# Loading the input batch by batch and re-planning the opening of a four-block transformer kernel on one core

## The chip, the cores and the metric

The kernel runs on one NeuronCore of a Trainium2 chip. TensorE (PE) multiplies matrices into PSUM; VectorE (DVE), ScalarE (ACT) and GpSimd (POOL) do the elementwise work; SyncE (SP) only issues DMA transfers. Each engine works off its own list of instructions in a fixed order and waits at semaphores. The metric is the device time of one execution in microseconds (us), lower is better.

## The reference, cut to what matters

The input `x` is (8, 256, 288): 8 batches of 256 tokens. Three transformer blocks follow each other, each with a condition vector `c` that gives six rows per batch (shift, scale and gate, twice), and a rotation closes:

```python
mod = silu(c) @ w_adaln + b_adaln                     # 6 rows of 288 per batch
sh_msa, sc_msa, g_msa, sh_mlp, sc_mlp, g_mlp = split(mod, 6)
h = ln(x) * (1 + sc_msa) + sh_msa
qkv = h @ w_qkv + b_qkv                               # 16 heads of 18
x = x + g_msa * (softmax(q k / sqrt(18)) v @ w_proj + b_proj)
h = ln(x) * (1 + sc_mlp) + sh_mlp
x = x + g_mlp * mlp(h)        # block 0: 4 experts, top 2; blocks 1 and 2: one MLP
...
U, _ = qr(P)                  # P is (288, 64)
R = expm(A(silu(c) @ W.T + b))# A skew-symmetric, 64x64, one per batch
out = x + ((x U) R - x U) U^T
```

Nothing before the second layer norm mixes batches, so batch 0 can go through its first attention while the input of batch 7 is still in HBM.

## The kernel before, in words

Activations stay in SBUF for the whole run: `X` holds the 16 tiles of 128 tokens (two tiles are one batch), `XT` the transposed and modulated copy as an f16 high part and an f16 low part. Weights are loaded as f32 into one of seven staging buffers (`STG`; four of them lie in the memory of `H`, so the trace calls them `H` early in the program), and ACT (`w_hi`, L2037 and L2042) and DVE (`w_lo`, L1679 and L1686) split them into high and low parts (`WQ`, `WP`, `WG`, `W`).

The program is written by a planner that runs when the kernel is built. Generators for the parts of the work (`prep`: layer norm, modulation, QKV; `maxima_rows`: row maxima of the scores, by DVE; `attend`; `settle` and `finish`; the MLP stream; `householder`: 64 reflections for the QR, one after another; `ada` and `vrows`: the rows from the condition vector) call `do(lane, kind, cost, ...)`, which appends a step to an engine's list. `deal` picks which generator goes on. Then `by_readiness` re-orders the steps of each engine: a model clock per engine, an assumed cost per step, and a tail after a step's end at which its result is there. For DMA steps this tail came from a table of constants, `LANDS` (6.0 us for a reload of saved weights, 7.5 us for `x_in`, 5.0 us for a weight block, 2.2 us for anything else), whatever else was in flight. On the chip only the resulting order counts.

The opening, with the lines of the trace: ACT's queue issues `x` in four transfers of two batches each (L2028). SP issues the condition vector (`c_in`, L2284), the first pair of 288-column groups of `w_adaln` (`cond_in`, L2292, bias L2295), `w_qkv` (`w_in`, L2306 to L2311), `P` transposed (`p_in`, L2287, tile `AT`), and the second pair of groups. PE's first instruction is the transposition of row 0 of the Householder reflections (L1566, reads `AT`), then the products of the condition rows (L1406), whose sums DVE adds (`cond_add`, L1673), PE transposes (L1399) and ACT copies to `SC` (L2062). POOL writes the identity and masks (`consts`), DVE writes constants in two steps: `xt_ones` (L1661 to L1667, which ACT's first activation waits for) and `dconsts` (L1638 to L1658: identity in f16, zeroed `QB`, `KB`, `WP1`, `V32`, columns of ones). The layer norm of a batch is BN_STATS (L1734) and BN_AGGR (L1739) on DVE, power on POOL, scaling on ACT (L2086, L2087), six transpositions on PE (L1416, L1417), modulation (`full`, L1715 on DVE) and split into `XT` (L1721 to L1730). The QKV products are L1389, seven f16 products per tile and third.

## Time and profile before

| | before |
|---|---|
| median of 3 runs | 1450.6 us (1448.38 to 1451.12) |
| the profiled execution's own time | 1447.77 us |
| its span in the trace | 1446.0 us |
| PE busy | 1337.2 us (92%) |
| DVE busy | 902.2 us (62%) |
| ACT busy | 788.8 us (55%) |
| POOL busy | 419.1 us (29%) |
| mean granted TensorE clock | 0.967 |

The span runs from the first to the last recorded instruction; the execution's own time has 1.8 us more around it. A busy PE counts a matmul at whichever clock was granted, so busy time is not work at full speed.

### The profile page before, as it was taken

The page shows a single profiled execution, that of the slowest core. Times are in us where ns is not written, and L with a number is a line of the kernel's source. Part 1 is how long each engine was busy: PE and PEld are TensorE (multiplying, and loading weights), DVE is VectorE, ACT ScalarE, POOL GpSimd, SP SyncE. Part 2 cuts the span into 40 slices and gives each one's busy share as a digit, 9 for nine tenths or more (in the row PEclk, how much of TensorE's full clock was granted, in tenths as well). Part 3 has the DMA queues.
Part 4 walks back from the last instruction along what each step waited for, and adds up shares of the span by engine and source line. Part 5 has one row for each costly group of instructions (what it writes and reads, how often), then busy time and mean ns, then how long its engine had stood idle before and what let it go on. Part 6 is the DMA issues. An engine that isn't in the chain of part 4 may idle for free.

```text
span 1446.0 us, 30299 instructions
## 1 busy us (share of the span) xinstructions
PE 1337.2 (92%) x11841; PEld 813.3 (56%) x11841; DVE 902.2 (62%) x1985; ACT 788.8 (55%) x1563; POOL 419.1 (29%) x805
## 2 busy tenths in 40 slices
PE   2777999899999999999999999989999999999978
PEld 1444555556567565665655665546656565555545
DVE  4678776776855655575447564584858755766442
ACT  2466677566754534454435343465655775755622
POOL 1213243242431334323343233221313323231110
PEclk8787999999999999999999999999999999999989
DMA  5114224534212312132212213141000130000000
GB/s 156 46 37 143 75 76 157 153 122 141 80 31 73 73 51 81 25 64 85 81 40 55 77 42 122 58 92 51 1 13 6 30 88 5 22 10 22 14 25 17
DMA packets 76738, 91.80 MB, mean 63 GB/s; under 512 B 38989, under 2 KB 69814, under 8 KB 73270
## 3 DMA queue, kind: packets, MB, share of 16 engines
q1 hardware_dynamic: 74486, 87.52, 20.8%
q10 hardware_dynamic: 2112, 2.36, 0.6%
q8 instruction: 94, 1.54, 0.4%
q14 instruction: 46, 0.38, 0.1%
HBM read 73.22 MB, written 16.38 MB: 62 GB/s over the span
## 4 chain that ended last, share of the span: by engine, by line
PE 79%; DVE 6%; issue 5%; ACT 4%; DMA 3%; SPq 2%; POOL 1%; POOLq 0%; DVEq 0%; ACTq 0%
PE P L1389 33%; PE P L1549 7%; PE P L1550 7%; PE P L1551 7%; PE P L1518 4%; DVE NM L1819 3%; PE P L1509 2%; PE P L1566 2%; PE P L1416 2%; PE P L1485 2%; PE P L1406 2%; PE P L1494 1%; PE P L1546 1%; PE P L1472 1%; PE P L1560 1%
## 5 line engine op out<-in xcount | busy, mean ns | idle before, releaser
L1389 PE MATMUL P<-XT,W 128*128 128x512 f16 x1512 | 350.7, 383 | 7.6 <-DVE XT L1730 4.8
L2246 POOL TENSOR_TENSOR X<-X,TM 128x288 f32<-128x288 f32 x144 | 123.6, 860 | 532.6 <-DVE TM L1894 340.8
L1549 PE MATMUL P<-W,H 128*128 128x288 f16 x864 | 248.3, 287 | 0.4 <-issue 0.3
L1550 PE MATMUL P<-W,H 128*128 128x288 f16 x864 | 248.0, 287 | 0.0
L1551 PE MATMUL P<-W,H 128*128 128x288 f16 x864 | 248.0, 287 | 0.0
L1389 PEld LDWEIGHTS P<-XT,W 128*128 128x128 f16 x1512 | 141.3, 98 | 179.7 <-issue 22.8
L2165 ACT ACTIVATE G<-P 128x512 f32<-128x512 f32 x216 | 128.9, 597 | 140.5 <-PE P L1389 131.0
L2155 ACT ACTIVATE ARENA<-P 128x512 f32<-128x512 f32 x256 | 136.0, 599 | 102.8 <-PE P L1509 102.1
L1819 DVE TENSOR_REDUCE NM<-P 128x2 f16<-128x512 f32 x256 | 159.9, 687 | 11.1 <-PE P L1494 10.5
L1389 PE MATMUL P<-WQ,XT 128*128 128x288 f16 x1008 | 143.9, 295 | 10.2 <-issue 5.3
L1888 DVE TENSOR_TENSOR H<-G,H 128x512 f16<-128x512 f32 x139 | 97.9, 708 | 85.3 <-ACT H L2166 85.2
L2251 POOL TENSOR_TENSOR H<-G,H 128x512 f16<-128x512 f32 x77 | 93.2, 1214 | 184.1 <-ACT H L2166 183.7
L2166 ACT ACTIVATE H<-P 128x512 f16<-128x512 f32 x216 | 128.5, 595 | 0.0
L1389 PEld LDWEIGHTS P<-WQ,XT 128*128 128x128 f16 x1008 | 96.6, 100 | 49.2 <-issue 21.3
L1549 PEld LDWEIGHTS P<-W,H 128*128 128x128 f16 x864 | 84.7, 98 | 27.7 <-issue 7.6
L1551 PEld LDWEIGHTS P<-W,H 128*128 128x128 f16 x864 | 84.7, 98 | 21.5
L1550 PEld LDWEIGHTS P<-W,H 128*128 128x128 f16 x864 | 84.7, 98 | 20.9
L2171 ACT ACTIVATE HQS<-P 64x288 f32<-64x288 f32 (+31 forms) x64 | 23.9, 374 | 119.8 <-PE P L1566 119.8
L1894 DVE SCALAR_TENSOR_TENSOR TM<-P,CW,G 128x288 f32<-128x288 f32 x64 | 32.9, 514 | 65.1 <-PE P L1551 64.7
L1518 PE MATMUL P<-ARENA,V 128*32 128x256 f32 x1024 | 71.3, 388 | 0.4 <-ACT ARENA L2155 0.3
L2080 ACT ACTIVATE FULL<-P,SC 128x256 f32<-128x256 f32 (+1 forms) x90 | 43.5, 557 | 41.2 <-PE P L1417 41.2
L1566 PE MATMUL P<-AT,IDF 64*64 64x288 f32 (+42 forms) x128 | 44.0, 426 | 23.7 <-DMA AT<-in_PT 16.9
(306 smaller groups left out, 2170.2 us busy)
## 6 DMA issues: line engine op xcount, KB each, us to landing
W<-scr_w SPq DMA_DIRECT2D x9, 1440.0 KB, 6.1
W<-scr_w SPq DMA_DIRECT2D x9, 1368.0 KB, 5.8
scr_w<-W SPq DMA_DIRECT2D x4, 1440.0 KB, 5.7
scr_w<-W SPq DMA_DIRECT2D x4, 1368.0 KB, 5.7
STG<-in_L_w SPq DMA_DIRECT2D x8, 576.0 KB, 5.1
STG<-in_L_w SPq DMA_DIRECT2D x9, 432.0 KB, 4.5
STG<-in_L_WT SPq DMA_DIRECT2D x11, 324.0 KB, 4.3
G<-scr_ada SPq DMA_DIRECT2D x24, 144.0 KB, 3.6
```

What stands on the lines that cost most here:

```text
L1389: ins = e.matmul(o, l, r, start=k == 0, stop=k == len(pairs_) - 1)
L1518: ins = e.matmul(bank(st)[32 * i:32 * i + 32, at], V32[u][:, kt, 4 * g + i, :], E32[s][:, i, kt * 256:(kt + 1) * 256], start=kt == 0, stop ...
L1549: e.matmul(o, hi, W2[:, 2 * m, :], start=False, stop=False)
L1550: e.matmul(o, hi, W2[:, 2 * m + 1, :], start=False, stop=False)
L1551: ins = e.matmul(o, lo, W2[:, 2 * m, :], start=False, stop=m == 8)
L1819: e.tensor_reduce(NM[:, :, st["par"], st["c"]], bank(st).rearrange("p (n k) -> p n k", n=2), AX.X, ALU.max, negate=True).then_inc(st.sem)
L1888: e.tensor_tensor(H[:, m, 1, :], G32[st["gi"]][:, :], H[:, m, 0, :], ALU.subtract).then_inc(st.sem)
L2155: e.activation(E32[st["s"]][:, st["h"], :], bank(st), ACT.Exp).then_inc(st.sem)
L2165: e.activation(G32[st["gi"]][:, :], bank(st), fn, scale=1.0 / WS)
L2166: e.activation(H[:, st["m"], 0, :], bank(st), fn, scale=1.0 / WS).then_inc(st.sem)
L2246: e.tensor_tensor(X[:, t, :], X[:, t, :], TM[st["k"]][:, :], ALU.add).then_inc(st.sem)
L2251: e.tensor_tensor(H[:, m, 1, :], G32[st["gi"]][:, :], H[:, m, 0, :], ALU.subtract).then_inc(st.sem)
```

## The change

What it does, part by part:

- Input. `x` comes in eight transfers of one batch (288 KB each, `x_in`, now also known to SP). ACT's queue issues batch 0 alone; SP issues batches 1 to 3 behind `w_qkv`, and each later batch `b + 3` when the planner begins to prepare batch `b` of block 0.
- Constants. DVE's first step is now only `zeros` (CS and PLUS). The ones rows of `XT`, the zeroed `V32` with its ones columns, and `WP1` are written by POOL (`xt_ones`), behind its masks. `dconsts` on DVE loses those and is the only kind in `LATE`: it gets an index that puts it behind every other step that is ready at the same model time. `consts` is costed at 3.2 us where it was 8.0.
- Reflections. `householder` waits until batch 0's Q and K of block 0 are transposed; `p_in` moves with it.
- Transfers in the planner. `LANDS` is gone. `Wire` is one clock for all DMA: a transfer starts when the earlier ones are through or 0.2 us after its issue, moves `SIZES` KB at 270 KB per us, and lands 1.6 us later. Issue costs of `cond_in` and `w_in` go up from 0.1 us to 0.45 to 1.85 us.
- At the entry of block 2, `attend` waits until none of block 1's exponent buffers (`rE1`) is held.

```diff
+class Wire:
+    def __init__(self):
+        self.clock = 0.0
+
+    def land(self, kb, issue):
+        self.clock = max(self.clock, issue + 0.2) + kb / 270
+        return max(self.clock + 1.6, issue + 2.1)
...
-            st.index, st.end = k, None
+            st.index, st.end = k + 100000 * (st.kind in LATE), None
...
-        consts = do(pool, "consts", 8.0, incs=1)
-        xt_ones = do(dve, "xt_ones", 2.5)
-        dconsts = do(dve, "dconsts", 2.0, after=consts)
+        consts = do(pool, "consts", 3.2, incs=1)
+        zeros = do(dve, "zeros", 0.4)
+        xt_ones = do(pool, "xt_ones", 5.5, incs=7)
+        dconsts = do(dve, "dconsts", 4.4, after=consts)
         c_in = do(sp, "c_in", 0.1, incs=16)
-        x_in = [do(act, "x_in", 0.1, incs=16, raises=f"x_in{q}", q=q) for q in range(4)]
...
+        def x_load(lane, b):
+            if b < B and not XW[2 * b]:
+                XW[2 * b] = XW[2 * b + 1] = [do(lane, "x_in", 0.45, incs=16, raises=f"x_in{b}", b=b)]
+
+        x_load(act, 0)
+        silu = do(act, "silu", 0.5, src=c_in, zero=zeros)
...
             if L:
                 yield from ms.wait(L - 1, b)
+            else:
+                x_load(sp, b + 3)
...
         def householder():
+            while ("turned", 0, 0) not in tok:
+                yield "wait"
             p_in = do(sp, "p_in", 0.1, incs=16)
...
             if L == 2 and b == 0:
+                while any(f is None for f in rE1.free):
+                    yield "wait"
...
+            def xt_ones(st):
+                q.wait_ge(consts)
+                e.memset(XT[96:128, 2, :], 0.0).then_inc(st.sem)
+                q.wait_ge(st.at(1))
+                e.memset(XT[96:98, 2, :], 1.0).then_inc(st.sem)
+                q.wait_ge(st.at(2))
+                for i in range(2):
+                    e.memset(V32[i][:, :, :, :], 0.0).then_inc(st.sem)
+                q.wait_ge(st.at(4))
+                for i in range(2):
+                    e.memset(V32[i][:, :, :, 18:19], 1.0).then_inc(st.sem)
+                e.memset(WP1[:, :, :], 0.0).then_inc(st.sem)
```

The order of PE's first instructions before: one reflection, both pairs of condition products, then batch 0's transpositions (L1416), another reflection, the third pair.

```order
L1566 MATMUL P<-AT,IDF 64x288
L1406 MATMUL P<-STG,CS 32x288 x6
L1406 MATMUL P<-H,CS 32x288 x6
...
L1416 MATMUL P<-IDF,ARENA 128x128 x2
L1417 MATMUL P<-IDF,ARENA 32x128
L1566 MATMUL P<-AT,IDF 64x287
L1406 MATMUL P<-STG,CS 32x288 x6
L1389 MATMUL P<-WQ,XT 128x288 x28
```

And PE's first instructions after the change (lines are about 31 further down in the changed file):

```order
L1437 MATMUL P<-STG,CS 32x288 x6
L1430 MATMUL P<-IDF,OSM 128x64 x2
L1430 MATMUL P<-IDF,OSM 32x64
L1447 MATMUL P<-IDF,ARENA 128x128 x2
L1448 MATMUL P<-IDF,ARENA 32x128
...
L1437 MATMUL P<-H,CS 32x288 x6
L1430 MATMUL P<-IDF,OSM 128x64 x2
L1430 MATMUL P<-IDF,OSM 32x64
L1420 MATMUL P<-WQ,XT 128x288 x28
```

No reflection stands before the QKV products any more, and the third pair of condition products has moved behind them, to just ahead of the row maxima of batch 0.

DVE before, from its first sum of condition rows on: the constants stand between the two BN_STATS of batch 0.

```order
L1673 SCALAR_TENSOR_TENSOR OSM<-P,PLUS,STG 64x288
L1679 SCALAR_TENSOR_TENSOR WQ<-STG,WQ 128x576
L1734 BN_STATS ST<-X 128x6
L1639 CAST IDH<-IDF 128x128
L1640 MEMSET WP 128x1152
...
L1657 MEMSET V_1 128x32
L1739 BN_AGGR MV<-ST 128x2
L1734 BN_STATS ST<-X 128x6
L1739 BN_AGGR MV<-ST 128x2
L1679 SCALAR_TENSOR_TENSOR WQ<-H,WQ 128x288
```

DVE after the change, around its last constant:

```order
L1690 MEMSET ONES 1x128
L1697 SCALAR_TENSOR_TENSOR OSM<-P,PLUS,STG 64x288
L1758 BN_STATS ST<-X 128x6
L1703 SCALAR_TENSOR_TENSOR WQ<-STG,WQ 128x288
L1703 SCALAR_TENSOR_TENSOR WQ<-STG,WQ 128x576
L1763 BN_AGGR MV<-ST 128x2
L1758 BN_STATS ST<-X 128x6
L1703 SCALAR_TENSOR_TENSOR WQ<-H,WQ 128x288
L1703 SCALAR_TENSOR_TENSOR WQ<-H,WQ 128x576
L1710 SCALAR_TENSOR_TENSOR WQ<-H,WQ 64x288
L1763 BN_AGGR MV<-ST 128x2
```

The constants stand ahead of the first condition sum, and three splits of `WQ` from staging buffers in `H` stand between the second BN_STATS of batch 0 and its BN_AGGR.

SP before, from the gate weights of block 0 on (`QT<-MT` is a batch's row of maxima, `G<-scr_ada` its gate row, `W` the first expert's weights):

```order
L2306 DMA STG<-in_L_w 128x1152 x2
L2340 DMA QT<-MT 1x8x256
L2341 DMA QT<-MT 1x8x256
L2330 DMA G<-scr_ada 128x288
L2309 DMA H<-in_L_w 32x1152 x3
L2311 DMA H<-in_L_b 32x1152
L2322 DMA scr_w<-W 128x5760
L2316 DMA H<-in_L_w 128x3x288
```

SP after the change, the same place:

```order
L2328 DMA X<-in_x 128x2x288
L2347 DMA STG<-in_L_w 128x1152 x2
L2350 DMA H<-in_L_w 32x1152 x3
L2352 DMA H<-in_L_b 32x1152
L2363 DMA scr_w<-W 128x5760
L2357 DMA H<-in_L_w 128x3x288
L2359 DMA H<-in_L_b 128x288
L2381 DMA QT<-MT 1x8x256
L2382 DMA QT<-MT 1x8x256
```

The row of maxima of batch 1 no longer stands ahead of the last third of the first expert's first matrix, its saving and the first part of its second matrix, but behind them.

## Rows read from the trace of the kernel before

**Rows 1.** stretches of the span: busy us (instructions) by engine, granted clock, DMA share, GB/s.

```profile
0.00:42.00 42.00, 13.22 (x53) 5.23 (x54) 20.44 (x58) 8.67 (x22) 8.43 (x35) 0.81 0.50 143
42.00:165.00 123.00, 95.06 (x880) 53.27 (x881) 91.67 (x203) 71.87 (x152) 31.46 (x80) 0.83 0.24 71
165.00:1100.00 935.00, 909.36 (x8263) 561.17 (x8260) 590.65 (x1322) 507.54 (x1018) 301.83 (x576) 0.99 0.25 73
1100.00:1300.00 200.00, 194.85 (x1705) 119.43 (x1702) 132.83 (x263) 135.30 (x246) 59.11 (x86) 1.00 0.10 28
1300.00:1446.00 146.00, 124.68 (x948) 74.17 (x946) 66.56 (x141) 65.37 (x126) 18.24 (x28) 0.93 0.07 19
```

**Rows 2.** timeline of PE: start us, us, what, count, idle before.

```profile
16.92 1.19 PE L1566 MATMUL P<-AT,IDF 64*64 64x288 f32 x2 [16.92 <-DMA AT<-in_PT]
...
33.26 0.58 PE L1399 MATMUL P<-IDF,OSM 64*128 64x64 f32 x3 [9.51 <-DVE OSM L1673]
...
38.88 3.10 PE L1406 MATMUL P<-STG,CS 96*32 96x288 f32 x12 [2.06 <-issue]
41.91 4.21 PE L1389 MATMUL P<-WQ,XT 128*128 128x288 f16 x28
...
50.55 1.19 PE L1494 MATMUL P<-KT,QT 64*128 64x256 f16 x16
...
127.10 1.04 PE L1494 MATMUL P<-KT,QT 64*128 64x256 f16 x8 [3.24 <-ACT HQS L2172]
...
165.11 1.67 PE L1389 MATMUL P<-XT,W 128*128 128x512 f16 x7
```

**Rows 3.** chain of waits, one piece between 30 and 45 us.

```profile
34.56 3.29 DMA STG<-in_L_b_adaln
```

**Rows 4.** DMA view of the first 17 us: volume, queues, issues with us to landing.

```profile
DMA packets 3830, 4.69 MB, mean 276 GB/s; under 512 B 536, under 2 KB 3446, under 8 KB 3830
...
q10 hardware_dynamic: 2070, 2.32, 46.4%
q1 hardware_dynamic: 1760, 2.37, 45.9%
...
STG<-in_L_w_adaln SPq DMA_DIRECT2D x2, 324.0 KB, 6.4
...
H<-in_L_w_qkv SPq DMA_DIRECT2D x1, 432.0 KB, 9.6
...
AT<-in_PT SPq DMA_DIRECT2D x1, 72.0 KB, 10.4
```

**Rows 5.** DMA queues between 137 and 145 us: packets, MB, share of 16 engines' span.

```profile
q1 hardware_dynamic: 957, 2.25, 90.0%
```

**Rows 6.** timeline of ACT.

```profile
4.75 1.28 ACT L2032 ACT_TABLE_LOAD   x1 [4.75 <-DVE XT L1667]
...
32.93 0.63 ACT L2086 ACTIVATE ARENA<-X,RS 128x288 f32<-128x288 f32 x1 [0.41 <-POOL RS L2230]
```

**Rows 7.** timeline of DVE.

```profile
26.67 0.91 DVE L1648 MEMSET V<- 128x1024 f32 x1 [0.16 <-issue]
...
30.36 0.18 DVE L1739 BATCH_NORM_AGGREGATE MV<-ST 128x2 f32<-128x6 f32 x1
30.46 1.11 DVE L1679 SCALAR_TENSOR_TENSOR WQ<-H,WQ 128x288 f16<-128x288 f32 x2
...
35.72 1.43 DVE L1715 TENSOR_SCALAR FULL<-P,SC 128x256 f32<-128x256 f32 x3 [0.90 <-PE P L1417]
...
38.97 0.22 DVE L1730 COPY XT<-XT 32x256 f16<-32x256 f16 x1
```

**Rows 8.** groups by line and form, one of POOL: busy us, mean ns.

```profile
L2254 POOL MEMSET EX<- 128x512 f32 x1 | 0.5, 517 | 0.0
```

**Rows 9.** tile AT: ns min/median/max, first and last start us.

```profile
L1945 DVE SCALAR_TENSOR_TENSOR AT<-HQS,HS,AT x64: 445/477/1378, 33.9 to 898.0; 64x288 f32<-64x288 f32 x1, 64x287 f32<-64x287 f32 x1, 64x286 f32<-64x286 f32 x1, 64x285 f32<-64x285 f32 x1
```

**Rows 10.** line L1625, the last product of the rotation, as rows 9.

```profile
L1625 PE MATMUL P<-STG x32: 402/403/844, 1244.1 to 1442.1; 64*128 64x288 f32 x32
```

More of the change, by code:

```diff
@@ L25 @@
 LAT, FILL, TAB = 0.08, 0.15, 1.3
[L26 removed]
+SIZES = dict(x_in=295, w_in=442, cond_in=345, w2_in=442, w_back=1400, w_keep=1400, g1_in=147, g2_in=295, tv_in=295, tv_out=295, out=295, v_in=640, wp1_in=350, p_in=74)
 AHEAD = 3
 NEAR = 0.1
+LATE = ("dconsts",)
 TABLES = dict(exps="exp", t_exp="exp", g_exp="exp", gelu="gelu", silu="silu")
@@ L122, in two, with by_readiness @@
     return slots(ring, 2)
-def by_readiness(lanes):
+def by_readiness(lanes, lands):
     queues, table = [], None
@@ L155, in by_readiness @@
         lane.clock = begin + st.cost
-        st.end = lane.clock + st.tail
+        st.end = lands(st, lane.clock)
         lane.steps.append(st)
@@ L185, in sem, with lands @@
             return sems[name]
+        wire = Wire()
+        def lands(st, at):
+            return wire.land(st.kb, at) if st.kb else at + (FILL if st.lane is pe else 0.0)
         pe, dve, act, pool, sp = (Lane(n) for n in ("pe", "dve", "act", "pool", "sp"))
@@ L195, in do @@
             lane.clock = max(lane.clock, max((ends(v) for v in fields.values() if isinstance(v, (Step, list))), default=0.0) + LAT) + cost
-            st.end = lane.clock + (LANDS.get(kind, 2.2) if incs >= 16 else FILL if lane is pe else 0.0)
+            st.kb, st.lane = SIZES.get(kind, 8) if incs >= 16 else 0, lane
+            st.end = lands(st, lane.clock)
             newest[0] = max(newest[0], st.end)
-            st.cost, st.tail, st.deps = cost, st.end - lane.clock, [x for v in fields.values() if isinstance(v, (Step, list, tuple)) for x in flat(v) if isinstance(x, Step)]
+            st.cost, st.deps = cost, [x for v in fields.values() if isinstance(v, (Step, list, tuple)) for x in flat(v) if isinstance(x, Step)]
             lane.steps.append(st)
@@ L435, in wp_load @@
             if L == 1:
-                tok["wp", L] = [do(sp, "wp1_in", 0.1, incs=80, w=I[w], bias=I[b], zero=dconsts)]
+                tok["wp", L] = [do(sp, "wp1_in", 0.1, incs=80, w=I[w], bias=I[b], zero=xt_ones)]
                 yield
@@ L1351, in program @@
         deal([Line(householder(), 4), loads, attends, ends_, tops, preps, bg, *(Line(rotated(k), 5) for k in range(2))])
-        by_readiness([pe, dve, act, pool, sp])
+        wire.clock = 0.0
+        by_readiness([pe, dve, act, pool, sp], lands)
         block = ctx.enter_context(nc.Block())
@@ L1635, in _, with zeros @@
             q = Waits(e)
+            def zeros(st):
+                e.memset(CS[:, :, :], 0.0)
+                e.memset(PLUS[:, :], 0.0)
+                e.drain()
+                e.memset(PLUS[0:32, 0:1], 1.0)
+                e.memset(PLUS[32:64, 1:2], 1.0).then_inc(st.sem)
             def d_consts(st):
@@ L1639, in d_consts @@
                 e.tensor_copy(IDH[:, :], IDF[:, :])
-                e.memset(WP1[:, :, :], 0.0)
                 e.memset(EV4[:, :], 0.0)
@@ L1646, in d_consts @@
                 e.memset(ONES[:, :], 0.0)
-                for i in range(2):
-                    e.memset(V32[i][:, :, :, :], 0.0)
                 e.drain()
@@ L1655, in d_consts @@
                 e.memset(ONES[32:33, :], 1.0)
-                for i in range(2):
-                    e.memset(V32[i][:, :, :, 18:19], 1.0)
                 e.drain().then_inc(st.sem)
-            def ones_rows(st):
-                e.memset(CS[:, :, :], 0.0)
-                e.memset(PLUS[:, :], 0.0)
-                e.memset(XT[96:128, 2, :], 0.0)
-                e.drain()
-                e.memset(PLUS[0:32, 0:1], 1.0)
-                e.memset(PLUS[32:64, 1:2], 1.0)
-                e.memset(XT[96:98, 2, :], 1.0).then_inc(st.sem)
             def cond_add(st):
```

27 lines of the change are left out of this document (14 added, 13 removed).

## The prediction

> **What bounds the kernel now.** I read first the table of stretches, because a change to the opening can only pay where PE is not already full. From 165 to 1300 us PE is busy 1104.2 of 1135 us, at a clock of 0.99 or 1.00 [rows 1]: whatever happens there, time is matmul work. Before 165 us it is different: PE is idle 28.8 of the first 42 us and 27.9 of the next 123, at a mean clock of 0.81 and 0.83 [rows 1]. The last 146 us are looser too (21.3 us idle), but the last 60 or so rows of PE's order are the same in both kernels. So the question is by how much the first expert product, at 165.11 us [rows 2], comes sooner, and whether what follows stays as dense.
>
> Then the timelines of the opening. PE's first instruction waits 16.92 us for `AT`, the reflections' input, and the condition products stand behind it [rows 2]. Next PE waits 9.51 us for DVE, which is writing constants between the two statistics of batch 0 (one V32 memset is shown at 26.67) [rows 2, 7]. Then batch 0 is normalised (ACT at 32.93), modulated (DVE 35.72) and complete in `XT` at 39.19, but the QKV products start only at 41.91, because the third pair of condition products, fed by a transfer that lands at 37.85, stands in front of them for 3.10 us [rows 2, 3, 6, 7]. Row maxima start at 50.55 [rows 2].
>
> **The input.** In the first 17 us 4.69 MB arrive, in two nearly equal halves: ACT's queue q10 (all of it `x`) 2.32 MB, SP's q1 2.37 MB [rows 4]. Nothing moves in about the first 2 us, so the rate is 4.69 / 15 = 0.31 MB per us (an estimate from that row). After the change 1.04 MB must land for the first condition products (condition vector, one pair of groups with biases, batch 0 of `x`): 2 + 3.4 = 5.4 us; with half a microsecond for the last transfer's own latency I take 6.0. For all of `w_qkv` it is 2.37 MB: 2 + 7.6 = 9.6 us. Before, its 432 KB block in `H` took 9.6 us from an issue at 4 us, and the first `w_adaln` group of a pair 6.4 us at the median [rows 4]. Batches 1 to 3 and the second pair, 1.6 MB more, are in by 15 us. ACT's first activation now waits for the condition vector and for a 0.1 us memset instead of the memset that ended at 4.7: done by 5 us with its table load of 1.28 [rows 6], ahead of the 6.0.
>
> **The opening, step by step.** PE: condition products 6.0 to 9.1 (3.10 for twelve [rows 2]; before they began behind the reflection at 18). DVE adds by 9.7, PE transposes by 10.3 (0.58 [rows 2]). DVE meanwhile: its constants. They filled some 7 us of PE's 9.51; less three long memsets of 0.9 to 1.0 and their pauses that leaves 3.5 to 4 [rows 2, 7], from 3.3 on (POOL's masks), so all before 7.5 us and hidden by the wait for data; without that cover they would cost those 3.5 to 4. From 9.7: statistics 0.44, two splits 1.2, AGGR and statistics 0.55, then the three splits that now stand in front of the last AGGR. They wait for ACT (high parts done at 11.7 and 12.4) and take 1.1 for two at 30.46 [rows 7] plus 0.5: AGGR at 13.4. From AGGR (30.36) to ACT's scaling (32.93) it was 2.6 us [rows 6, 7], so scaling starts at 16.0, ends at 17.1, PE's six transpositions end at 18.7, and modulation starts there. From 35.72 to the end of the COPY at 39.19 it took 3.5 us [rows 7]; now the second condition sum stands inside and waits for PE's second block (18.7 to 21.8): 1.4 us more. `XT` is ready and QKV starts at **23.7** instead of 41.91: 18.2 us.
>
> POOL's new memsets: 512 f32 elements took 517 ns [rows 8], 1 ns each. Two of 2048 f16, two of 1024 and one of 1152 are 7300 elements, 7.3 us, from 3.3 to 10.6; with EX and UT behind them 11.5, and POOL is wanted at 13.4: no cost. If the f16 ones went by bytes it would be 8.5 to 9.5; if everything took twice as long, 18.7, and batch 0 would be 5.3 us later.
> [...] No row here shows a POOL memset of f16. [...]
>
> The third pair of condition products now stands behind QKV and ahead of the row maxima; its transfer is issued at about 23 and in by 28. QKV with its transpositions took 7.7 us (41.91 to 49.6), so maxima start at 23.7 + 7.7 + 1.7 to 3.1 = 33.1 to 34.5 instead of 50.55: 16 to 17.4 us.
>
> **From there to the first expert product.** The chain is the same: row maxima of batch 0, QKV of batch 1 beside attention of batch 0, maxima of batch 1, and so on, with DVE at 91.7 of 123 us and nearly full in the maxima [rows 1]. Gains and losses on it:
> - Reflections are moved, not removed. One at the head of batch 1's QKV costs 0.6 us at slow clock. Up to the first expert product there are 8 instead of 10; the two others land where PE is full, 2 x 0.7 = 1.4 us. One more block of `vrows` products (1.65 us) has been done by then, which comes off again.
> - The splits of the first expert's first matrix (two of 1.36 us) go into batch 1's maxima: -2.7 there, +2.7 before batch 2's.
> - SP no longer waits for batch 1's row of maxima before it issues the rest of those weights. PE's wait of 3.24 us at 127.10 comes from that: ACT stood at a split whose data had not landed, and batch 2 and a reflection behind it [rows 2]. Worth 0 to 5 us; I take 2.
> - x transfers in SP's queue cost 0.45 us of issue each, behind waits of SP at most 20 us before their batch is read: nothing.
>
> Sum at the first expert product: 16.7 + 2 - 0.6 = 18, bookkeeping of reflections and `vrows` about zero. **18 us**.
>
> **The rest.** The order of PE is nearly the same from 26% to 68% of the work. At the entry of block 2 it differs: the first scores of block 2 stand after 74.1% of the columns, where they stood after 71.8%, because block 1's last attention is later too. PE is busy 194.9 of 200 us there [rows 1], and fillers (the MLP of block 1) are at hand. I put this at 0, with -4 to +4 from about 50 us of idle time beyond 165 us [rows 1] that falls anew. The reflections end at 898 us and the first product that needs them starts at about 1240 [rows 9, 10]: a delay of 20 us has over 300 us of slack.
>
> The profiled execution took 1447.77 us; 1447.8 - 18 = 1429.8. The median of the runs is 2.8 us above that execution, so **1432.6 us**, 1.2% faster. Its own range: 18 us, less 3 (POOL or DVE late) and 4, plus 3 and 4, is 1426 to 1440.
>
> **Rivals.**
> - *The first data come no sooner*, because each queue has its own ceiling: q1 moved 2.37 MB in 15 us beside q10, 0.16 per us [rows 4]. Then `w_qkv` (2.07 MB on q1) is in at 15, batch 1 to 3 at 20.5, the second pair at 25. PE's second condition block starts at 25, QKV at 30: the gain shrinks by about 6, 1439. Against it: alone, q1 moved 2.25 MB between 137 and 145 us, 0.28 per us, with 90% of the engines' time [rows 5]. The Trainium skill (DMA: Bandwidth & Descriptors, "Issuing engines are not separate DMA queues") says the same: all queues run on the same 16 engines, and spreading issues over them saves only issue time. By it the shift of `x` to SP costs issue time and the order of bytes decides. Chance 0.10.
> - *More is gained*: with fewer waits PE also spends less time at the low clock. In the first 165 us the mean clock is 0.83; a stretch at half of 2.4 GHz doubles matmul time (28 QKV products took 4.21 us, of which the last ones ran fast). If a quarter of the 27.9 us idle between 42 and 165 us went (7), instead of the 2 counted above, and 1 to 5 us of slow matmuls with it, it is 24 to 28 us: 1420 to 1426. For it: the maxima of batch 1 now lie between scores. Against: DVE bounds those stretches. Chance 0.14.
> - *Slower than before: the entry of block 2.* There the first attention comes 2.3% of the work later, 0.023 x 1337 = 31 us. If PE ran out of other work at the end for that long, the end moves by up to 31 us and 18 are given back: 1463. It decides from 18 uncovered microseconds on. For it: the new guard at `attend`, and a tail that is already 21 us idle [rows 1]. Against: the last 5% of PE's order is the same in both, and the last row maxima stand at 93 to 94% in both. Chance 0.10: split 0.03 faster (1440 to 1447), 0.03 same, 0.04 slower.
> - The forecast itself: 0.66.
>
> **Range and chances.** 1426 to 1440 holds the forecast and the first rival; the second and third would need 1420 to 1463. Leaving out the far end of the third and a little of the second, 1422 to 1442. A measurement of this kernel tells 0.2% (3 us) from no change: faster 0.66 + 0.10 + 0.14 + 0.03 = 0.93, same 0.03, slower 0.04.
>
> **What the profile after would show.** Right: PE's first product at 5.5 to 6.5 us, no DVE wait of 9 us, QKV at 22 to 26, first row maxima at 32 to 36, first expert product at 145 to 149; from 1100 us on every milestone 16 to 20 us earlier, with the same density. POOL's memsets done before DVE's second AGGR. Wrong: QKV at 24 but the first expert product at 155 or later (then a wait took the place of those removed, SP's queue first); PE idle between 1080 and 1300 us well above 5 us (the entry of block 2); a first product at 9 us or later (the rate of a queue).

## The result, and the profile after the change

| | before | after |
|---|---|---|
| median | 1450.65 us (4 runs) | 1431.24 us (4 runs, 1426.82 to 1435.11) |
| the profiled execution's own time | 1447.77 us | 1433.26 us |
| its span | 1446.0 us | 1431.4 us |
| PE busy | 1337.2 us | 1338.2 us |
| mean granted TensorE clock | 0.967 | 0.971 |

The ratio of the medians is 0.9868, with a 95% interval of 0.9835 to 0.9902: 1.3% faster, where 1432.6 us was forecast. A second, independent set of runs of the changed kernel (after_again, below) gave 1432.15 us. The two profiled executions differ by 14.5 us and the medians by 19.4; against 17 more runs of before, made beside it, after_again's difference is 17.6. PE's busy time is the same within 1 us, so the span lost about 15 us of PE's idle time. The question is where.

The same stretches as in [rows 1], of the changed kernel: length, then busy us (instructions) of PE, weight load, DVE, ACT and POOL, granted clock, DMA share, GB/s.

```profile
0.00:42.00 42.00, 22.93 (x161) 12.64 (x162) 26.13 (x68) 13.39 (x31) 15.58 (x45) 1.00 0.47 129
42.00:165.00 123.00, 99.02 (x841) 53.69 (x840) 87.10 (x193) 77.52 (x160) 31.59 (x70) 0.79 0.33 94
165.00:1100.00 935.00, 914.52 (x8351) 565.75 (x8351) 583.10 (x1305) 514.72 (x1031) 309.77 (x589) 1.00 0.25 72
1100.00:1300.00 200.00, 190.91 (x1684) 116.21 (x1684) 138.11 (x279) 130.68 (x245) 49.80 (x73) 0.98 0.09 24
1300.00:1431.00 131.00, 110.85 (x813) 64.93 (x810) 60.12 (x126) 58.44 (x115) 20.89 (x30) 0.93 0.06 20
```

In the first 42 us PE now works 22.9 us instead of 13.2, and in the next 123 us 99.0 instead of 95.1. From 165 to 1100 it works 5.2 us more in the same 935 us, which the forecast did not have, and from 1100 to 1300 3.9 us less. The clock of 1.00 in the first row holds only for what was recorded, which begins at 28.1 us: the twelve condition products take 3.09 us at 7.56 and 1.65 us at 33.36 (below), so the first ran at the lower of the two levels, 1.2 GHz. In the second row PE is busy 4.0 us more than before, but with 841 products instead of 880 and at a clock of 0.79 instead of 0.83.

PE's timeline, the places that [rows 2] shows of before and a few more: start us, us, what, count, idle before.

```profile
7.56 3.09 PE L1437 MATMUL P<-STG,CS 96*32 96x288 f32 x12 [7.56 <-DMA STG<-in_L_w_adaln]
18.21 0.69 PE L1447 MATMUL P<-IDF,ARENA 128*128 128x128 f32 x2 [6.31 <-ACT ARENA L2111]
24.73 5.20 PE L1420 MATMUL P<-WQ,XT 128*128 128x288 f16 x28 [0.83 <-issue]
33.36 1.65 PE L1437 MATMUL P<-STG,CS 96*32 96x288 f32 x12
34.95 1.07 PE L1525 MATMUL P<-KT,QT 64*128 64x256 f16 x16
48.01 1.21 PE L1597 MATMUL P<-AT,IDF 64*64 64x287 f32 x2 [2.06 <-DVE AT L1969]
62.84 0.38 PE L1525 MATMUL P<-KT,QT 64*128 64x256 f16 x4
106.43 0.95 PE L1525 MATMUL P<-KT,QT 64*128 64x256 f16 x8 [1.43 <-ACT HQS L2196]
154.29 3.19 PE L1420 MATMUL P<-XT,W 128*128 128x512 f16 x7
```

Against [rows 2]: first product 9.4 us sooner, QKV 17.2, first row maxima 15.6, first expert product only 10.8. There is no 9.51 us wait for DVE any more; what is longest is 7.56 us for the first data and 6.31 us for batch 0's layer norm.

DVE and POOL in the opening.

```profile
3.30 1.91 DVE L1677 CAST IDH<-IDF 128x128 f16<-128x128 f32 x1 [1.92 <-POOL ID L2238]
6.06 1.02 DVE L1686 TENSOR_SCALAR KB<-SAME 128x128 f16<-128x128 f16 x2
7.16 0.17 DVE L1690 MEMSET ONES<- 1x128 f16 x1
10.69 0.51 DVE L1697 SCALAR_TENSOR_TENSOR OSM<-P,PLUS,STG 64x288 f32<-64x288 f32 x1 [3.37 <-PE P L1437]
```
```profile
3.33 1.80 POOL L2242 MEMSET XT<- 32x2048 f16 x1
5.19 1.80 POOL L2244 MEMSET XT<- 2x2048 f16 x1
10.56 0.33 POOL L2309 MEMSET UT<- 64x288 f32 x1
14.85 0.78 POOL L2256 TENSOR_SCALAR NMS<-MV 128x2 f32<-128x2 f32 x1 [3.95 <-DVE MV L1763]
```

DVE's constants are through at 7.3 us and DVE then idles 3.37 us for PE; POOL's memsets are through at 10.9 and POOL then idles 3.95 us. Both are covered, with 3 to 4 us to spare.

### The profile page after: what moved, and what is told of

Its sections match the earlier page's. It is cut to its first block, busy times and chain, and to the rows that moved or that the text cites. A ratio compares the mean times of both kernels' runs of the same rounds, so it can differ in the third digit from the quotient of the medians.

```text
span 1431.4 us, 30303 instructions
## 1 busy us (share of the span) xinstructions
PE 1338.2 (93%) x11841; PEld 813.2 (57%) x11841; DVE 894.6 (62%) x1967; ACT 794.8 (56%) x1580; POOL 427.6 (30%) x806
## 4 chain that ended last, share of the span: by engine, by line
PE 82%; DVE 8%; issue 5%; ACT 3%; DMA 1%; POOL 1%; SPq 0%; POOLq 0%; DVEq 0%; ACTq 0%
PE P L1420 35%; PE P L1580 7%; PE P L1581 7%; PE P L1582 7%; DVE NM L1843 4%; PE P L1549 4%; PE P L1540 2%; PE P L1597 2%; PE P L1516 2%; PE P L1447 2%; PE P L1437 2%; PE P L1525 1%; PE P L1591 1%; PE P L1577 1%; PE P L1503 1%
## 5 line engine op out<-in xcount | busy, mean ns | idle before, releaser
L2288 POOL TENSOR_TENSOR H<-G,H 128x512 f16<-128x512 f32 x80 | 98.4, 1231 | 161.6 <-ACT H L2190 156.3
L1581 PEld LDWEIGHTS P<-W,H 128*128 128x128 f16 x864 | 84.9, 98 | 21.4
L1447 PE MATMUL P<-IDF,ARENA 128*128 128x128 f32 x256 | 51.4, 297 | 20.9 <-ACT ARENA L2111 11.3
```

The lines of the kernel that those rows point to most:

```text
L1581: e.matmul(o, hi, W2[:, 2 * m + 1, :], start=False, stop=False)
L2288: e.tensor_tensor(H[:, m, 1, :], G32[st["gi"]][:, :], H[:, m, 0, :], ALU.subtract).then_inc(st.sem)
```

## The experiments

Three questions. What did each part of the opening give? Does a lead in the opening arrive at the end? And what is the order behind the opening worth, which the planner draws anew at every edit? To read the answers, PE's busy time up to a fixed instant is the ruler: of two kernels with the same work, the one that has 10 us more busy time by 165 us leads by 10 us there. The ruler has a fault: a product at the low clock takes about twice as long and counts about twice, and the totals of busy time lie between 1336.7 and 1343.9 us for the same products. So a second ruler stands beside it, an estimate from the same traces: busy time weighted with the clock granted at that moment, and with one half ahead of the first record of the clock (22.7 us before, 28.1 in the changed kernel, and each other kernel's own). Its totals agree better, 1302.4 to 1306.1 us. I call it the lead at full speed; two profiles of one kernel differ in it by about 2 us. The stretches of before and of the changed kernel, columns as above:

```profile
0.00:165.00 165.00, 108.28 (x932) 58.50 (x933) 112.11 (x261) 80.54 (x174) 39.89 (x115) 0.82 0.30 89
165.00:880.00 715.00, 701.38 (x6400) 430.62 (x6398) 453.13 (x1037) 388.93 (x798) 244.34 (x485) 0.99 0.27 81
880.00:1010.00 130.00, 119.04 (x1114) 76.02 (x1112) 72.56 (x152) 65.65 (x123) 32.21 (x52) 0.97 0.29 79
```
```profile
0.00:165.00 165.00, 121.95 (x1000) 66.33 (x1001) 113.23 (x260) 90.92 (x191) 47.17 (x115) 0.84 0.37 103
165.00:880.00 715.00, 696.76 (x6383) 428.46 (x6382) 446.28 (x1018) 390.85 (x803) 247.94 (x492) 1.00 0.27 79
880.00:1010.00 130.00, 128.48 (x1132) 80.99 (x1131) 87.62 (x188) 73.72 (x136) 36.38 (x60) 1.00 0.26 64
```

So by busy time the changed kernel leads by 13.7 us at 165, 9.1 at 880 (4.6 lost), 18.5 at 1010 (9.4 won), 14.6 at the end (3.9 lost). At full speed it is 8.6 us at 165, 5.3 at 880, 16.9 at 1010, and 14.6 at the end: some 9 us come from the opening, and some 6 from what lies behind it, above all between 880 and 1010 (in the second profile, after_again, 7 and 9). The same leads for all kernels, worked out in the same way from their own traces; the last column is the difference of the spans, and the ratios further down are against runs of before made beside each kernel (medians 1449.49 to 1450.65 us):

| kernel | median us | first product / QKV / row maxima | first expert product | lead by busy time at 165 / 880 / 1010 | lead at full speed (estimate) at 165 / 880 / 1010 | at the end |
|---|---|---|---|---|---|---|
| before | 1450.65 | 16.92 / 41.91 / 50.55 | 165.11 | 0 / 0 / 0 | 0 / 0 / 0 | 0 |
| changed kernel | 1431.24 | 7.56 / 24.73 / 34.95 | 154.29 | 13.7 / 9.1 / 18.5 | 8.6 / 5.3 / 16.9 | 14.6 |
| after_again | 1432.15 | 7.54 / 24.71 / 35.94 | 156.04 | 13.8 / 9.2 / 18.6 | 6.6 / 3.2 / 14.7 | 15.6 |
| x_all_act | 1438.02 | 10.44 / 27.62 / 38.76 | 158.79 | 10.4 / 5.2 / 14.7 | 4.0 / 0.4 / 12.0 | 9.4 |
| consts_back | 1443.00 | 7.52 / 25.37 / 38.05 | 153.18 | 12.4 / 12.9 / 12.9 | 8.9 / 12.3 / 11.0 | 4.9 |
| hh_later | 1446.95 | 7.40 / 24.58 / 34.45 | 153.74 | 10.5 / 9.0 / 7.3 | 10.2 / 8.2 / 4.7 | 0.0 |
| hh_first | 1441.40 | 7.02 / 25.09 / 35.20 | 143.79 | 16.5 / 9.1 / 12.7 | 16.1 / 8.6 / 14.3 | 9.2 |
| lands | 1448.26 | 7.57 / 26.37 / 38.63 | 152.07 | 7.6 / -3.5 / 2.7 | 9.8 / -8.0 / 0.3 | -3.1 |
| b_hh | 1457.72 | 10.50 / 35.40 / 44.67 | 160.90 | 4.4 / -0.2 / -3.0 | 1.1 / -0.7 / -7.1 | -8.3 |
| b_x | 1468.20 | 13.69 / 33.17 / 45.48 | 165.00 | 1.7 / -14.3 / -10.4 | -1.3 / -21.4 / -17.0 | -21.8 |
| rate_260 | 1451.27 | 7.23 / 23.89 / 35.30 | 153.95 | 14.2 / 5.9 / 4.2 | 9.8 / 1.0 / -0.3 | -1.2 |
| rate_280 | 1441.15 | 8.23 / 26.19 / 37.16 | 173.63 | 10.4 / 8.8 / 12.9 | 4.5 / 5.7 / 8.9 | 8.0 |
| tail_20 | 1438.27 | 7.11 / 23.93 / 35.43 | 151.25 | 13.9 / 8.9 / 13.1 | 13.7 / 11.5 / 14.4 | 10.2 |
| before_w2_55 | 1457.76 | 16.85 / 42.05 / 50.60 | 167.78 | -0.6 / -7.0 / -2.3 | -1.8 / -12.6 / -5.8 | -7.5 |

**after_again**: the changed kernel once more, without an edit.

> The changed kernel once more, unchanged, as the standard for the three others on the same chip. Expected: ratio to the kernel before 0.985 to 0.989, a profiled span within 4 us of 1431.4, QKV of batch 0 within 0.5 us of 24.73 and the first expert product within 2 us of 154.3 us. If the first expert product wanders by 3 us or more between two profiles of the same kernel, then a part of the 7 us by which it missed its predicted place is clock (0.79 of full speed between 42 and 165 us) and not order.

Measured: 1432.15 us, ratio 0.9878 [0.9864, 0.9893]. The first expert product came at 156.04 (154.29 in the other profile): 1.75 us of wandering, not 3. So the 7 us by which it missed its forecast place are not chance. The two executions differ by 1.0 us at the row maxima already, because the 28 QKV products took 5.20 us in one and 6.22 in the other.

**x_all_act**: the order of the changed kernel on every engine, the old flow of bytes (the first function is ACT's, the second SP's).

```diff
             def x_in(st):
-                b = st["b"]
-                e.dma_start(X[:, 2 * b:2 * b + 2, :], x_v[:, 2 * b:2 * b + 2, :]).then_inc(st.sem, 16)
+                for b in range(B):
+                    e.dma_start(X[:, 2 * b:2 * b + 2, :], x_v[:, 2 * b:2 * b + 2, :]).then_inc(sems[f"x_in{b}"], 16)
...
             def x_in(st):
-                b = st["b"]
-                e.dma_start(X[:, 2 * b:2 * b + 2, :], x_v[:, 2 * b:2 * b + 2, :]).then_inc(st.sem, 16)
+                pass
```

> The changed kernel with every engine's order as it is; only ACT's queue issues all eight transfers of x at its start and SP's issues none, so that x again takes half of the rate from the weights. Theory (the first data set the opening, and queues share one rate): the first condition products need 0.75 MB of SP's queue, which then have to be shared with as much of x, so they start at 8.5 to 10 us instead of 7.56, and w_qkv is in at 15 to 17 us instead of about 12; QKV of batch 0 starts 1 to 3 us later than at 24.7, and the time is 1 to 3 us above that of the changed kernel. Rival (the order of the instructions gives the gain, data rate is worth nothing): QKV at 24.7 and no difference within 1 us.

Measured: 1438.02 us, ratio 0.9922 [0.9909, 0.9935], so 5.9 us above after_again: the direction of the theory, but about twice the top of its 1 to 3 us. The first product came at 10.44 us (8.5 to 10 was expected), QKV 2.9 us later. The DMA view of its first 17 us, then the same of the changed kernel (packets, MB, share of 16 engines; issues with KB each and median us to landing):

```profile
q1 hardware_dynamic: 1814, 2.43, 47.5%
q10 hardware_dynamic: 2013, 2.19, 43.7%
...
STG<-in_L_w_adaln SPq DMA_DIRECT2D x2, 324.0 KB, 6.2
H<-in_L_w_qkv SPq DMA_DIRECT2D x1, 432.0 KB, 10.3
```
```profile
q1 hardware_dynamic: 3008, 3.70, 78.7%
q10 hardware_dynamic: 272, 0.29, 5.2%
...
STG<-in_L_w_adaln SPq DMA_DIRECT2D x2, 324.0 KB, 4.4
H<-in_L_w_qkv SPq DMA_DIRECT2D x1, 432.0 KB, 6.3
```

With x taken off ACT's queue SP's moved 3.70 MB instead of 2.43 in the same time: the rate is shared, and the ceiling of the first rival, 0.16 MB per us for one queue, is not there. The Trainium skill (DMA: Bandwidth & Descriptors, "Issuing engines are not separate DMA queues") has this rule, and the trace agrees. PE's first product, QKV and row maxima all came 2.8 to 3.8 us later, and with the order held, this delay was still there by busy time at 165 (3.2), at 880 (3.8) and at 1010 (3.8). At full speed it is 4.6, 4.9 and 4.9 against one profile of the changed kernel and 2.6, 2.8 and 2.7 against the other. This is the one experiment in which only the opening differs: **a lead in the opening does arrive at the end if the order behind it is the same**. It arrived as 5.2 and 6.2 us in the spans against the two profiles, and 5.9 in the medians; whether it grew on the way or the rulers are off by that much stays open.

**consts_back**: constants as before, on DVE.

```diff
-LATE = ("dconsts",)
+LATE = ()
...
-        consts = do(pool, "consts", 3.2, incs=1)
-        zeros = do(dve, "zeros", 0.4)
-        xt_ones = do(pool, "xt_ones", 5.5, incs=7)
-        dconsts = do(dve, "dconsts", 4.4, after=consts)
+        consts = do(pool, "consts", 8.0, incs=1)
+        xt_ones = do(dve, "xt_ones", 2.5)
+        dconsts = do(dve, "dconsts", 2.0, after=consts)
...
```

> The changed kernel with the constants as they were before: all memsets on DVE, POOL only its masks, no step held back to the end of ready ones. The planner then puts DVE's constants behind the first sum of condition rows and ahead of the first statistics. Theory (DVE's constants on the path of batch 0 cost their own length): 3.5 to 5 us of DVE in front of batch 0's normalisation, QKV at 28 to 30 instead of 24.7, time 3 to 5 us above the changed kernel. Rival (they fall in a wait for w_qkv or for the second statistics): QKV within 1 us of 24.7, time the same. Second rival: the delay is made up before the first expert product, by DVE's full stretch: QKV late by 4, first expert product and time late by under 1.5.

Measured: 1443.00 us, ratio 0.9959 [0.9946, 0.9972]. QKV was late by 0.6 us only, as the first rival had it, but PE then waited 0.71 us for the condition sum and 0.71 for `KT`, and row maxima began 3.1 us later. The second pair of condition products also moved ahead of batch 0's transpositions, so the constants are not all that differs. At 165 us 1.3 us of lead were missing by busy time and none at full speed (8.9 against 8.6 and 6.6). The 10.9 us that it lost in the medians against after_again are mostly not the constants: at 880 it led by 12.3 at full speed, 7 more than the changed kernel, and then lost 1.3 by 1010, where the changed kernel won 11.6, and 6.1 behind it.

**hh_later**: no reflection at the head of batch 1's QKV.

```diff
-            while ("turned", 0, 0) not in tok:
+            while ("turned", 0, 1) not in tok:
```

> The changed kernel, but the reflections begin only once batch 1 (not batch 0) is transposed: none stands at the head of batch 1's QKV. In the changed kernel PE waited 2.06 us for it there and ran it in 1.21. Theory A (that reflection is one of the waits that cost the opening its lead): QKV of batch 1 starts 1.5 to 3 us sooner than at 49.15, row maxima of batch 1 as much before 62.84, and the time is 1 to 3 us lower. Theory B (DVE bounds this stretch and PE has slack): maxima of batch 1 within 0.5 us of 62.84, and no difference in time beyond 1 us.

Measured: 1446.95 us, ratio 0.9982 [0.9968, 0.9996]: 14.8 us above after_again. PE's timeline at the place of the edit, then behind 940 us:

```profile
46.74 3.52 PE L1420 MATMUL P<-WQ,XT 128*128 128x288 f16 x14 [1.29 <-issue]
...
62.58 0.61 PE L1525 MATMUL P<-KT,QT 64*128 64x256 f16 x8 [0.55 <-DVE KT L1839]
...
946.93 0.55 PE L1602 MATMUL P<-IDF,UT 64*96 64x64 f32 x3 [3.57 <-DVE UT L1978]
```

Both halves of the question have an answer. At the edit, QKV of batch 1 came 2.4 us sooner (46.74 against 49.15), but batch 1's row maxima only 0.3: so the reflection there costs next to nothing, and that PE now waits 0.55 us for DVE's `KT` ahead of the maxima fits theory B's reason. And the time moved by 15 us all the same, far behind the edit: the last reflection now stood at 933 us instead of 893, and PE waits 3.57 us at 946.93 in the rotation's chain behind it. The lead fell from 9.0 at 880 to 7.3 at 1010 by busy time (8.2 to 4.7 at full speed), where the changed kernel won 9.4 (11.6). Neither theory had this.

**b_hh** and **b_x**: before with one part of the change each.

```diff
         def householder():
+            while ("turned", 0, 0) not in tok:
+                yield "wait"
```
```diff
-        x_in = [do(act, "x_in", 0.1, incs=16, raises=f"x_in{q}", q=q) for q in range(4)]
+        def x_load(lane, b):
+            if b < B and not XW[2 * b]:
+                XW[2 * b] = XW[2 * b + 1] = [do(lane, "x_in", 0.45, incs=16, raises=f"x_in{b}", b=b)]
+
+        x_load(act, 0)
...
+        x_load(sp, 1)
+        x_load(sp, 2)
```

> The kernel before with one part of the change: reflections wait until batch 0 is transposed (p_in moves with it). x still comes in four transfers of two batches on ACT's queue, DVE still writes all constants, LANDS stands. Expected: PE's first instruction is the condition product, at about 10.4 us as in x_all_act (which has the same flow of data), 7.7 us sooner than behind the reflection (18.1); QKV of batch 0 at 33 to 35 instead of 41.91. Theory A (the opening sets the time): 7 to 8 us faster than before, ratio 0.995. Theory B (what the planner makes of the rest counts for as much): the last reflection stands at 64.6% of PE's work and the rotation's chain up to 74%, as in hh_later and consts_back, which idled 12.6 and 13.1 us between 885 and 1010 us; before idles 10.9 there, and from 1010 us on hh_later is like before. So by B the gain of the opening shrinks to 0 to 4 us, ratio 0.997 to 1.000.

> The kernel before with the other part alone: x batch by batch, batch 0 on ACT's queue and the others on SP's behind w_qkv (LANDS has 3.5 us for x_in instead of 7.5). PE still begins with a reflection, so it waits for AT, which SP loads behind w_qkv: with x out of the way AT's 72 KB are in at 2.9 MB by 0.32 MB per us, about 11 to 12 us instead of 16.92. Theory A (the opening sets the time): first product 5 us sooner, QKV 3 to 5 us sooner, 3 to 5 us faster, ratio 0.9965 to 0.998. Theory B (the planner's rest): the row maxima of the first block stand elsewhere (the last block's entry comes at 79% of PE's work instead of 70%), and the time moves by 5 us or more in either direction from what A gives.

Measured: b_hh 1457.72 us, ratio 1.0041 [1.0023, 1.0059]; b_x 1468.20 us, 1.0122 [1.0096, 1.0149]. Both start sooner (first product 10.50 and 13.69, QKV 35.40 and 33.17; b_hh's QKV was expected at 33 to 35, b_x's first product at 11 to 12 and its QKV at 37 to 39), and both end later than before, b_x by 17.6 us. At 165 us their leads were 4.4 and 1.7 by busy time, but 1.1 and -1.3 at full speed: of these two openings next to nothing was left there. b_x then lost 20 us by 880; b_hh lost 1.8 by 880 and 6.4 between 880 and 1010. Of theory B the direction held, and for b_x the size (5 us or more); b_hh came out slower than its range. Theory A failed in both.

**lands**: the changed kernel with the old table of landing times in the planner.

```diff
-            return wire.land(st.kb, at) if st.kb else at + (FILL if st.lane is pe else 0.0)
+            return at + LANDS.get(st.kind, 2.2) if st.kb else at + (FILL if st.lane is pe else 0.0)
...
```

> The changed kernel with the planner's old table LANDS in place of the shared clock Wire; all else as changed. In the opening PE then has both pairs of condition products ahead of the transpositions of batch 0, and the third pair in the middle of QKV. Theory A: QKV starts at 21.5 to 25 us (the second pair is not between the transpositions and QKV, but its data come at about 15 to 17 us) and is held once by the third pair; at the row maxima it stands within 2 us of the changed kernel, and so does the time. Theory B (the planner's rest): the time is 3 to 10 us above the changed kernel, with the loss behind 800 us and not in the opening.

Measured: 1448.26 us, ratio 0.9983 [0.9966, 1.0001], 16.1 us above after_again. PE's timeline:

```profile
16.96 3.10 PE L1438 MATMUL P<-H,CS 96*32 96x288 f32 x12 [5.06 <-DMA H<-in_L_w_adaln]
...
26.37 3.52 PE L1421 MATMUL P<-WQ,XT 128*128 128x288 f16 x14 [3.72 <-issue]
```

With the table the planner puts the second pair ahead of batch 0's transpositions, PE waits 5.06 us for its data, QKV starts at 26.37 (21.5 to 25 was expected) and row maxima come 3.7 us late. By 165 us that was made up. By busy time the kernel is 6.1 us short there, but it ran at a mean clock of 0.90 where the changed kernel had 0.84; at full speed it leads by 9.8 us, more than the changed kernel, and the first expert product comes at 152.07, 2.2 us sooner. It then lost 17.8 us between 165 and 880. So theory B holds as to the place, behind the opening, though sooner than 800 us, and the loss is larger than its 3 to 10 us. That `Wire` is worth something by its order in the opening is not shown.

**rate_260**, **rate_280**, **tail_20**, and **before_w2_55** for before: nothing but one constant of the planner is changed, so that PE's order in the opening stays and the order behind it is drawn anew, as if by lot; I call each such order a draw.

```diff
-        self.clock = max(self.clock, issue + 0.2) + kb / 270
+        self.clock = max(self.clock, issue + 0.2) + kb / 260
```

That is rate_260; rate_280 has 280 there, and tail_20 has `self.clock + 2.0` instead of 1.6 in the line behind it. In before_w2_55 `w2_in=6.0` of `LANDS` is 5.5.

> The changed kernel with Wire's rate at 260 KB per us in the planner instead of 270. Nothing on the chip changes by it but the order that the planner writes: PE's first 554 rows are the same, so the opening and the first expert product are the same (within 1.5 us), and behind them the order is drawn anew. This measures what the order behind the opening is worth by itself. Theory A (the opening alone is the gain, the rest is equal in sum): within 2 us of the changed kernel. Theory B: 3 us or more apart, and the difference lies in the idle time of PE between 880 and 1010 us (1.5 us in the changed kernel, 10.9 before) or behind 1150.

> The changed kernel with Wire's rate at 280 KB per us instead of 270: PE's first 104 rows are the same, the rest of the order is drawn anew. With rate_260 (19 us above the changed kernel with the same opening) this and tail_20 tell whether the changed kernel's rest is a lucky draw or rate_260's an unlucky one. Lucky: both land at 1443 to 1455 us, like rate_260, hh_later, consts_back and lands, with 10 us or more of PE's idle time between 880 and 1010 us in at least one. Unlucky: both at 1428 to 1437.

> The changed kernel with Wire's tail behind a transfer at 2.0 us instead of 1.6: PE's first 364 rows are the same, the rest is drawn anew. As for rate_280: 1443 to 1455 us if the changed kernel's rest is a lucky draw, 1428 to 1437 if it is a common one. The first expert product within 2 us of 154.3 to 156.0 in either case.

> The kernel before with 5.5 us instead of 6.0 for w2_in in LANDS: PE's first 527 rows are the same as before's, the rest is drawn anew. This is the draw for before. If draws of either opening scatter by 5 to 10 us, it lies 3 us or more from 1450.5. If before's own order was a good draw, as the two partial kernels b_hh (1457.7) and b_x (1468.2) suggest, which both began sooner and ended later, it comes out slower, 1453 to 1468; if the sooner opening is worth its 11 us at the first expert product on equal draws, the mean of the draws of before's opening lies 8 to 12 us above that of the draws of the changed opening.

Measured: rate_260 1451.27 us, 1.0008 [0.9992, 1.0025]; rate_280 1441.15, 0.9939 [0.9916, 0.9962]; tail_20 1438.27, 0.9918 [0.9893, 0.9943]; before_w2_55 1457.76, 1.0052 [1.0032, 1.0072]. rate_260 has the opening of the changed kernel in PE's rows, led by 14.2 us at 165 by busy time (9.8 at full speed), and was no faster than before. Its stretches:

```profile
0.00:165.00 165.00, 122.44 (x1009) 66.97 (x1010) 113.89 (x263) 91.50 (x193) 47.35 (x115) 0.86 0.37 104
165.00:880.00 715.00, 693.08 (x6339) 423.89 (x6337) 447.76 (x1013) 386.34 (x795) 250.52 (x493) 0.99 0.26 77
880.00:1010.00 130.00, 117.34 (x1117) 75.26 (x1119) 74.77 (x159) 64.97 (x121) 29.43 (x49) 0.99 0.30 79
```

The largest piece is between 880 and 1010 us, where the second MLP block ends, the chain of small f32 products of the rotation runs, and block 2 enters: 11.1 us of busy time less than in the changed kernel. What PE waits for there (us in total, times, longest), first of rate_260, then of the changed kernel:

```profile
PE P L1577 <- DVE W L1721: 1.8, 1, 1.8
PE P L1611 <- DVE OSM L1992: 1.7, 1, 1.7
PE P L1577 <- DVE TM L1918: 1.6, 1, 1.6
PE P L1420 <- issue: 1.4, 1, 1.4
...
```
```profile
PE P L1471 <- DVE KT L1801: 0.7, 1, 0.7
PE P L1420 <- issue: 0.6, 1, 0.6
PE P L1420 <- DVE XT L1754: 0.3, 1, 0.3
```

Not one wait, but some fifteen small ones. In the changed kernel those steps lie between other products and block 2's QKV runs from 924 us on.

Of the expectations, "a lucky draw" had 1443 to 1455 for rate_280 and tail_20, "an unlucky one" 1428 to 1437; they came at 1441.15 and 1438.27, between the two. The four orders behind the changed opening give 1431.7 (mean of its two medians), 1438.3, 1441.2 and 1451.3, mean 1440.6; the changed kernel is the best of them. The two behind before's opening give 1450.7 and 1457.8, mean 1454.2. The difference of the means is 13.6 us, but with a scatter of 8 us over four draws and 5 over two it is uncertain by some 5 us. It agrees with an opening whose lead, 4.5 to 13.7 us at 165 at full speed, arrives at the end; it does not measure it.

**hh_first**: the changed kernel with the reflections from the start.

```diff
-            while ("turned", 0, 0) not in tok:
-                yield "wait"
```

> The changed kernel without the wait of the reflections: SP loads AT right behind w_qkv, PE runs one reflection between the first condition sums and the transpositions of batch 0, and a second one just ahead of QKV. Theory A (they cost the opening time): AT is in at about 12 us, the first reflection lies in PE's wait for ACT, but the second waits for DVE's update of AT, so QKV starts 1 to 4 us later than 24.7, and row maxima as well. Rival: both lie in waits and QKV starts within 0.5 us of 24.7. The time cannot tell them apart, since the rest is drawn anew: 1435 to 1460 us.

Measured: 1441.40 us, ratio 0.9937 [0.9914, 0.9961].

```profile
13.16 1.22 PE L1595 MATMUL P<-AT,IDF 64*64 64x288 f32 x2 [1.80 <-DMA AT<-in_PT]
17.67 0.69 PE L1445 MATMUL P<-IDF,ARENA 128*128 128x128 f32 x2 [3.29 <-ACT ARENA L2109]
...
23.67 0.69 PE L1595 MATMUL P<-AT,IDF 64*64 64x287 f32 x2 [0.84 <-DVE AT L1967]
25.09 5.10 PE L1418 MATMUL P<-WQ,XT 128*128 128x288 f16 x28 [0.72 <-issue]
```

QKV at 25.09 against 24.73 (24.71): by its own words the rival holds. But the first product came 0.54 us sooner here, at 7.02, so counted from there QKV is 0.9 us later (18.1 us against 17.2). In the kernels that begin with the same condition products the first one wanders from 7.02 to 8.23 us, and differences under a microsecond in the opening are not to be read without it. Once the condition products stand ahead of it, the first reflection lies in PE's wait for ACT, and at 165 us this kernel even led by 16.5 us (16.1 at full speed), with the first expert product at 143.79. So holding the reflections back until batch 0 is transposed gained at most that 0.9 us; what counts is that none stands ahead of the condition products. Which edit of the planner brings that about was not isolated.

No version here beats the changed kernel. Not isolated either is the wait of block 2's entry (the guard on `rE1`): taking it away alone was not tried, since ACT and DVE would then write one buffer with nothing to order them. hh_later, consts_back and rate_260 have it too and do not share what the changed kernel wins from 880 to 1010 us, so it does not make that gain by itself. What it is worth when added alone to before stays open.

## Why the prediction was right, and which of its steps were not

- **The opening** was right to 1.6 us. First product at 7.56 instead of 6.0 (5.5 to 6.5 was forecast; 9 would have meant a queue's ceiling): the data start later than I took. Constants on DVE done at 7.3 (forecast 7.5) and POOL's at 10.9 (11.5). QKV at 24.73 against 23.7, row maxima at 34.95 against 33.1 to 34.5: 15.6 us sooner, forecast 16 to 17.4.
- **What the constants cost**: hidden, as forecast; without the cover 3.1 us at the row maxima (3.5 to 4 was forecast) and nothing that the full-speed ruler shows at 165 (consts_back).
- **The stall behind `w2`** shrank: PE's wait of 3.24 us at 127.10 [rows 2] has its nearest like in one of 1.43 at 106.43. It was priced at 2, bounds 0 to 5.
- **The first expert product** failed: 154.29 instead of 147, 10.8 us sooner instead of 18 (9.1 in after_again); by the prediction's own test ("155 or later") this was on the edge. The lead at full speed, 8.6 and 6.6 us, says the same. The step that failed is the sum 16.7 + 2 - 0.6, which carried the lead at the row maxima through to this product. From the row maxima to the first expert product, before and then in the changed kernel:

```profile
50.55:165.11 114.56, 86.62 (x803) 46.85 (x803) 84.92 (x185) 66.48 (x142) 28.93 (x74) 0.82 0.24 73
34.95:154.29 119.34, 92.23 (x821) 49.08 (x820) 87.00 (x186) 70.17 (x150) 30.69 (x72) 0.80 0.29 87
```

That is 119.34 us instead of 114.56. It was not a wait in place of those removed: PE's idle time is 27.1 us instead of 27.9. PE is busy 5.6 us longer. At full speed it did 75.1 us of work instead of 73.5, so 1.6 us are more work ahead of that product, and the other 4.0 are slower clock. The prediction had no term for the clock in its sum; it stood in a rival, as a gain. As a milestone the product is right in most kernels, but in rate_280 it stood at 173.63 while that kernel led by 4.5 us at full speed, because the planner had moved other work ahead of it.

- **"The rest" at 0 with -4 to +4** was wrong too. Behind 165 us the changed kernel won 6.0 us more (14.6 less 8.6), and 9.0 in after_again. With one constant changed it loses 11.0 (rate_260), and over all kernels here that begin with the condition products on the new flow of `x`, the rest is worth between -12.9 (lands) and +9.0. With such bounds faster could not have stood at 0.93: rate_260 with this opening, and hh_later and lands too, were within 0.2% of before.
- **So the number was near by luck.** The opening gave 9 us less than forecast, this draw of the rest gave 6 us more, and the medians happen to lie 19.4 us apart where the two profiled executions lie 14.5.
- **The rivals.** *A queue's own ceiling*: refuted by q1's 3.70 MB. *More gained*: not here, but hh_first shows 16.1 us at 165; its range was also put too low, for 24 to 28 us off 1450.6 is 1423 to 1427 and not 1420 to 1426. *Block 2's entry*: a part was there: from 1100 to 1300 us PE idled 9.1 us instead of 5.2. The mechanism that I priced (uncovered work at the end) was not what made b_hh and b_x slower: b_x lost 20 us at full speed between 165 and 880, b_hh 6.4 between 880 and 1010. "The change slows it" deserved more than 0.04, on the ground of the reordering and not of one place.

The planner's own clock is a weak guide among its orders. Its end for PE, a model's figure and no measured one, stands here beside the medians. Ends worked out with `LANDS` and with `Wire` come from two models, so they are compared only within a group:

```
LANDS           planner's end   median
b_hh                1386.4      1457.72
before_w2_55        1387.2      1457.76
before              1389.7      1450.65
lands               1395.3      1448.26
b_x                 1396.5      1468.20

Wire            planner's end   median
consts_back         1392.8      1443.00
changed             1393.3      1431.24
rate_280            1396.8      1441.15
hh_later            1400.6      1446.95
hh_first            1403.8      1441.40
tail_20             1404.1      1438.27
rate_260            1405.6      1451.27
```

Among the four orders with one opening and `Wire` (changed, rate_280, tail_20, rate_260) it picks the best and the worst rightly; with the others the order breaks.

## What to carry to other kernels

Where a planner or scheduler writes the order, an edit of the opening also draws the whole rest anew. Here the draws behind one opening lay 20 us apart, and the opening's own lead was some 7 to 9 us: measure the edit with the order held, or over several draws, before believing its sign or its size. Follow a lead by PE's busy time up to fixed instants, but weight it with the granted clock, or slow products count as lead; a named instruction agrees with it unless the scheduler moves work past it. And several draws with one constant moved a little are themselves a cheap way to a better kernel.
